# Softmax sums by three adding transfers a group in rotating buffers, with two small operations moved between engines

## The reference, cut to what matters

```python
q = (query @ Wq).reshape(b, sq, 32, 32).transpose(0, 2, 1, 3)
k = (key @ Wk).reshape(b, sk, 8, 32).transpose(0, 2, 1, 3)     # 8 heads, each serves 4 of q
v = (value @ Wv).reshape(b, sk, 8, 32).transpose(0, 2, 1, 3)
scores = jnp.einsum('bhqd,bhkd->bhqk', q, k) * scale            # 512 queries x 1024 keys a head
probs = jax.nn.softmax(scores, axis=-1)
out = jnp.einsum('bhqk,bhkd->bhqd', probs, v)
return out.transpose(0, 2, 1, 3).reshape(b, sq, 1024) @ Wo
```

## Time and profile before

| | us |
|---|---|
| median of 3 runs | 1242.94 (1241.52 to 1243.02) |
| the profiled execution | 1241.61 |
| its span, first to last instruction | 1239.8 |
| TensorE busy | 1208.2 (97%) |
| VectorE busy | 781.4 (63%) |
| GpSimd busy | 682.0 (55%) |
| ACT busy | 488.0 (39%) |
| mean granted clock of TensorE | 0.994 |

### The profile page before, as it was taken

The page is one execution under the profiler, slowest core; times in us unless marked ns, Lnnn a source line. Parts: engine busy times, 40 slices in busy tenths (PEclk is TensorE's granted clock), DMA queues, the critical chain, the costliest instruction groups (busy, mean ns, idle before and its releaser), DMA issues.

```text
span 1239.8 us, 16842 instructions
## 1 busy us (share of the span) xinstructions
PE 1208.2 (97%) x6358; PEld 511.8 (41%) x6440; DVE 781.4 (63%) x1303; ACT 488.0 (39%) x879; POOL 682.0 (55%) x300
## 2 busy tenths in 40 slices
PE   8999799999999999999999999999999999999998
PEld 6664344444444322222323233234444444444443
DVE  8898731433456788887878888145559846737622
ACT  4787421000110477776777777743252010010000
POOL 6006996500082188988999899860165543524500
PEclk9999899999999999999999999999999999999999
DMA  9577233311361145564656464533474343523301
GB/s 354 176 253 187 68 123 98 86 35 34 78 192 60 35 101 125 113 127 106 131 116 130 107 131 97 112 77 60 102 225 139 121 136 102 180 75 103 118 17 51
DMA packets 94302, 145.12 MB, mean 117 GB/s; under 512 B 54672, under 2 KB 64912, under 8 KB 90128
## 3 DMA queue, kind: packets, MB, share of 16 engines
q1 hardware_dynamic: 59712, 99.51, 25.8%
q0 software_dynamic: 4608, 33.56, 13.5%
q10 hardware_dynamic: 29904, 11.02, 4.0%
HBM read 89.16 MB, written 10.60 MB: 80 GB/s over the span
## 4 chain that ended last, share of the span: by engine, by line
PE 71%; POOL 11%; DMA 10%; DVE 5%; issue 2%; ACT 1%; SPq 0%; POOLq 0%; DVEq 0%; ACTq 0%
PE bank L706 48%; POOL R L672 7%; DMA stage_pair<-R 5%; PE bank L975 5%; PE bank L962 5%; PE bank L1007 4%; PE bank L1050 4%; DMA R<-R 3%; PE bank L755 3%; PE bank L724 2%; POOL stage_pair L672 2%; POOL xn L654 1%; DVE lnv L1548 1%; DMA XTl<-xn 1%; DMA stage_c<-ctx_t_in 0%
## 5 line engine op out<-in xcount | busy, mean ns | idle before, releaser
L1782 DVE TENSOR_REDUCE mxp<-bank 128x1 f32<-128x512 f32 x512 | 323.2, 683 | 86.1 <-PE bank L962 84.2
L1416 ACT ACTIVATE R<-bank 128x512 f32<-128x512 f32 x512 | 271.9, 602 | 107.9 <-PE bank L1050 103.2
L706 PE MATMUL bank<-XTh,R 128*128 128x512 bf16 x878 | 274.5, 380 | 3.2 <-DVE X L1830 2.3
L672 POOL TENSOR_TENSOR R<-R 128x2048 f32<-128x2048 f32 x48 | 222.3, 4631 | 79.1 <-ACT R L1416 51.1
L706 PE MATMUL bank<-R 128*128 128x512 bf16 x941 | 208.0, 379 | 1.1
L706 PE MATMUL bank<-XTl,R 128*128 128x512 bf16 x436 | 165.6, 380 | 0.8 <-issue 0.2
L694 POOL TENSOR_TENSOR R<-stage_pair,R 128x1024 bf16<-128x1024 f32 x32 | 75.7, 2382 | 130.0 <-DVE R L1940 69.4
L706 PEld LDWEIGHTS bank<-R 128*128 128x128 bf16 x960 | 93.9, 98 | 113.3
L975 PE MATMUL bank<-R,stage_c 128*32 128x512 f32 x1024 | 136.4, 604 | 0.7 <-ACT R L1416 0.7
L1050 PE MATMUL bank<-R 98*128 98x512 bf16 x352 | 133.9, 381 | 1.2 <-DVE R L1810 0.8
L962 PE MATMUL bank<-R 96*128 96x512 bf16 x352 | 134.4, 382 | 0.0
(11 more groups left out here) (202 smaller groups left out, 1428.3 us busy)
## 6 DMA issues: line engine op xcount, KB each, us to landing
stage_pair<-wts_in SPq DMA_DIRECT2D x35, 512.0 KB, 3.6
R<-R POOLq DMA_DIRECT2D x16, 1024.0 KB, 7.5
stage_pair<-R POOLq DMA_DIRECT2D x16, 1024.0 KB, 7.0
stage_pair<-w_in SPq DMA_DIRECT2D x32, 512.0 KB, 3.5
stage_c<-w_in SPq DMA_DIRECT2D x32, 512.0 KB, 3.6
R<-q_scr SPq DMA_DIRECT2D x48, 128.0 KB, 2.5
XTh<-ctx_t_in SPq DMA_DIRECT2D x11, 512.0 KB, 7.0
XTh<-ctx_nat_in SPq DMA_DIRECT2D x9, 512.0 KB, 4.2
```

Of the source, the lines that this page charges most:

```text
L672: pool.tensor_tensor(PS[(0, 1, 2, 1)[j]], PB[2 * j % 4], PB[2 * j % 4 + 1], ALU.add).then_inc(p_add, 1)
L706: mm = pe.matmul(o, a, m, start=first and a is ah and bs is bh, stop=last and a is al)
L1416: act.activation(PB[kt % 4][:, h * S:(h + 1) * S], bank[t_bank(g, t)][:, :], ACT.Exp, scale=float(HD) ** -0.5).then_inc(exp_done, 1)
L1782: dve.tensor_reduce(mxp[head // REP % 2][:, m, n // 2, n % 2:n % 2 + 1], bank[s_bank(u)][:, :], AX.X, ALU.max).then_inc(s_max, 1)
```

## The change: what it does

Sum buffers. The first buffer of a group, `total_in(g)`, is PS[0] for even groups; for odd groups it is a free stretch of another tensor (XTh's half of batch 1 for groups 1, 3, 5, 7, eight pieces of 1 KB a partition; half of `V` for 9 to 15). PS[1] and PS[2] take turns as `beside(g, 0)` and `beside(g, 1)`. Adds 0, 1, 2, 3 write total, beside 0, beside 1, beside 0. There are three adding transfers, all onto the total: the first after add 1, the second (of beside 1) just ahead of add 3, the third (of beside 0) after add 0 of the next group. So TensorE needs one product with ones a group, at step 30 of the next group; the last group still has two.

Moves. The copy of the values goes from GpSimd to ACT (step 12). The lower part goes from GpSimd to VectorE (step 10, for the group three before), the upper part from step 28 to step 4 of the next group. `divide` comes after add 2. `sums_in` is put behind the loads of the queries and keys in SP's queue, and `invert_few` goes from step 8 to 14. `junk`, a place for unused results, moves in `V`. The last three lower parts stay on GpSimd.

```diff
-TOTAL_AT = (2, 18)
-SUM_OUT_AT = 20
-FEW_AT = 8
-O_HI_AT = 28
+TOTAL_AT = 30
+SUM_OUT_AT = 31
+FEW_AT = 14
+O_HI_AT = 4
+VALUES_AT = 12
+O_LO_AT = 10
...
+        xth_1 = per_tile(XTh[:, :].bitcast(F32))[:, :, B * S // 4:B * S // 2]
...
+        def pieces(v):
+            return v.rearrange("p (k n) -> p k n", k=KT)
+        def total_in(g):
+            if g % 2 == 0:
+                return pieces(PS[0])
+            return xth_1 if g < KV_HEADS else pieces(V[:, 0:REP * S])
+        def beside(g, i):
+            return pieces(PS[1 + (g + i) % 2])
...
             for g in range(1, GROUPS):
                 rows_in(g)
-                if g >= 2:
-                    sums_in(g - 2)
                 if g + 2 < GROUPS:
                     sp.wait_ge(st_mm, STEPS * g)
                     queries_in(g + 2)
                     keys_in(g + 2)
+                if g >= 2:
+                    sums_in(g - 2)
...
+            def add_pair(g, j):
+                pool.wait_ge(exp_done, STEPS * g + 2 * REP * (j + 1))
+                if j == 0:
+                    if g >= 2:
+                        pool.wait_ge(one_mm, g - 1)
+                    dst = total_in(g)
+                elif j == 1:
+                    if g > 0:
+                        pool.wait_ge(ps_c, 16 * g)
+                    dst = beside(g, 0)
+                elif j == 2:
+                    if g > 0:
+                        pool.wait_ge(ps_d, 16 * g)
+                    dst = beside(g, 1)
+                else:
+                    pool.wait_ge(ps_b, 16 * (g + 1))
+                    dst = beside(g, 0)
+                pool.tensor_tensor(dst, pieces(PB[2 * j % 4]), pieces(PB[2 * j % 4 + 1]), ALU.add).then_inc(p_add, 1)
             for g in range(GROUPS):
                 for j in range(KT // 2):
-                    pool.wait_ge(exp_done, STEPS * g + 2 * REP * (j + 1))
                     if j == 3:
-                        pool.wait_ge(ps_sum[0], 16 * (g + 1))
-                    elif g > 0 and j == 1:
-                        pool.wait_ge(ps_sum[1], 16 * g)
-                    elif g > 0:
-                        pool.wait_ge(one_mm, 2 * (g - 1) + j // 2 + 1)
-                    pool.tensor_tensor(PS[(0, 1, 2, 1)[j]], PB[2 * j % 4], PB[2 * j % 4 + 1], ALU.add).then_inc(p_add, 1)
-                    if j % 2 == 1:
-                        pool.wait_ge(p_add, 4 * g + j + 1)
-                        pool.dma_start(PS[j - 1], PS[1], accum_op=ALU.add).then_inc(ps_sum[j // 2], 16)
-                    if j == 0 and 1 <= g < GROUPS - 1:
-                        stage_values(g + 1)
-                    if g >= 2 and j == 1:
+                        pool.wait_ge(p_add, 4 * g + 3)
+                        pool.wait_ge(ps_b, 16 * (g + 1))
+                        if g + 1 < GROUPS:
+                            pool.dma_start(total_in(g), beside(g, 1), accum_op=ALU.add).then_inc(ps_c, 16)
+                    add_pair(g, j)
+                    if j == 0 and g > 0:
+                        pool.wait_ge(p_add, 4 * g)
+                        pool.wait_ge(ps_c, 16 * g)
+                        pool.dma_start(total_in(g - 1), beside(g - 1, 0), accum_op=ALU.add).then_inc(ps_d, 16)
+                    if j == 1:
+                        pool.wait_ge(p_add, 4 * g + 2)
+                        pool.dma_start(total_in(g), beside(g, 0), accum_op=ALU.add).then_inc(ps_b, 16)
+                    if j == 3 and g + 1 == GROUPS:
+                        pool.wait_ge(p_add, 4 * GROUPS)
+                        pool.dma_start(beside(g, 1), beside(g, 0), accum_op=ALU.add).then_inc(ps_d, 16)
+                    if g >= 2 and j == 2:
                         divide(g - 2)
-                    if g >= 2 and j == 2:
-                        divided_lo(g - 2)
+            divided_lo(GROUPS - 3)
...
+            def over_pieces(weights, probs, first, last):
+                n = KT // REP
+                for h in range(REP):
+                    mm = pe.matmul(bank[6][h * HD:(h + 1) * HD, :].rearrange("p (k n) -> p k n", k=n), weights,
+                                   probs[:, h * n:(h + 1) * n, :], start=first, stop=last)
+                return mm
...
-            def total(g, j):
-                pe.wait_ge(ps_sum[j], 16 * (g + 1))
-                if j == 0 and g > 0:
+            def total(g):
+                if g > 0:
                     pe.wait_ge(sum_out, g)
-                over_keys(bank[6], onesf[:, 0:HD], PS[2 * j], j == 0, j == 1).then_inc(one_mm, 1)
+                if g + 1 < GROUPS:
+                    pe.wait_ge(ps_d, 16 * (g + 1))
+                    over_pieces(onesf[:, 0:HD], total_in(g), True, True).then_inc(one_mm, 1)
+                else:
+                    pe.wait_ge(ps_b, 16 * GROUPS)
+                    over_pieces(onesf[:, 0:HD], total_in(g), True, False)
+                    pe.wait_ge(ps_d, 16 * GROUPS)
+                    over_pieces(onesf[:, 0:HD], beside(g, 1), False, True).then_inc(one_mm, 1)
...
+            def values_staged(g):
+                act.wait_ge(pv_mm, KT * (g - 1))
+                b, kv = divmod(g, KV_HEADS)
+                src = V[:, b * KT * KVD:(b + 1) * KT * KVD].rearrange("p (t n) -> p t n", t=KT)
+                act.activation(VS[g % 2].rearrange("p (t n) -> p t n", t=KT), src[:, :, ds(kv, HD)], ACT.Copy).then_inc(vs_done, 1)
...
-                    if g > 1 and t == O_HI_AT:
-                        divided_hi(g - 2)
+                    if g > 2 and t == O_HI_AT:
+                        divided_hi(g - 3)
+                    if 1 <= g < GROUPS - 1 and t == VALUES_AT:
+                        values_staged(g + 1)
...
+            def divided_lo(g):
+                cols = o_cols(g)
+                dve.wait_ge(o_hi, g + 1)
+                dve.tensor_tensor(XTl[:, cols], onat, XTh[:, cols], ALU.subtract).then_inc(o_lo, 1)
...
+                    if g > 2 and t == O_LO_AT:
+                        divided_lo(g - 3)
```

More of the change, by code:

```diff
@@ L217, in build @@
         b2b = xn[0]
-        junk = V[:, 0:D // 2].bitcast(BF16)
+        junk = V[:, B * KT * KVD // 2:B * KT * KVD // 2 + D // 2].bitcast(BF16)
         stage_e = stage_w + stage_c
@@ L311, in build @@
         p_add = sem("p_add")
-        ps_sum = [sem(f"ps_sum{i}") for i in range(2)]
+        ps_b = sem("ps_b")
+        ps_c = sem("ps_c")
+        ps_d = sem("ps_d")
         one_mm = sem("one_mm")
@@ L634, in stage_values @@
             def stage_values(g):
-                if g >= 2:
-                    pool.wait_ge(pv_mm, KT * (g - 1))
                 b, kv = divmod(g, KV_HEADS)
@@ L1058, in group @@
                             weigh(g - 1, KT - 1)
-                    if g > 0 and t in TOTAL_AT:
-                        total(g - 1, TOTAL_AT.index(t))
+                    if g > 0 and t == TOTAL_AT:
+                        total(g - 1)
                     if STEPS * g + t >= STEPS * GROUPS - 6 * KT:
@@ L1096, in _ @@
             output_tile(1)
-            total(GROUPS - 1, 0)
-            total(GROUPS - 1, 1)
+            total(GROUPS - 1)
             pe.wait_ge(o_out, GROUPS)
@@ L1401, in sums_out @@
             def sums_out(g):
-                act.wait_ge(one_mm, 2 * (g + 1))
+                act.wait_ge(one_mm, g + 1)
                 if g > FEW_GROUPS:
@@ L1438, in _ @@
                 exp_group(g)
+            divided_hi(GROUPS - 3)
             outputs_out(GROUPS - 1)
```

## The result

The changed kernel takes 1296.9 us (median of 4 runs, 1291.7 to 1301.2) against 1243.0 (1241.5 to 1243.1) for the kernel before: ratio 1.0439, 95% interval 1.0411 to 1.0466. It is slower, as forecast and by the mechanism forecast, but by 54 us instead of 20: outside the range of 1234 to 1277. (Rival C of the prediction has numbers up to 1310, but from issues of 7 us and stalls of 4.6, and neither came; that the result lies there is chance.) The profiled execution took 1297.05 us, its span is 1295.2.

A forecast was written before the change was run, and what follows sets the result against it. TensorE, busy 97% of the span, was taken as the bound, GpSimd next. From 1241.6 us the terms -12.9 - 3 - 1 + 36.3 + 1 = +20.4 gave 1262.0; the 8-in-10 range was 1234 to 1277.

The forecast's parts named there:

- Rival C: GpSimd late but not enough, stalls of 4.6 us giving 1277; or issues in pieces dear, up to 1310; 7%.
- Rival A: VectorE's lower part at step 10 isn't held up and costs little: 1231 us; 10%.
- The clock behind the stalls: After step 13 of groups 3 to 13 TensorE idles some 3.3 us, its granted clock still full.
- The stall, 3.3 a group: TensorE stands 3.3 us while VectorE's lower part is held by addition 0, groups 3 to 13: +36.3 us.
- Rival B: GpSimd runs late, so VectorE's lower part falls between additions 3 and 0, unheld: 1235 us; 10%.
- Yes, on time, with 0.2 to spare: With the stall, GpSimd still finishes addition 3 just before the next group's addition 0 is due.
- Products with ones, -12.9: On TensorE in the attention loop, 15 products with ones saved at 0.86 us each: -12.9 us.
- Excess of the long windows, -3: Of 3.8 us by which four attention groups run long, rotating buffers remove 3 (between 0 and -3.8).
- "I take nothing" for the pieces: Adding transfers into 1 KB pieces, odd groups below 8, cost nothing extra to issue; high end 7 us.
- SyncE's order, 0: Moving `sums_in` behind the loads on SP's queue costs 0, the reciprocals landing with 1.3 us of cover.
- The two ends, -1 and +1: The last `total` no longer waits for a late transfer, -1 us; group 14's turn of maxima comes later, +1.
- Values on ACT, upper part: Copying values on ACT at step 12 costs 0; the upper part at step 4 makes exp(7) 0.2 us late.

The follow-up runs named there:

- e5: The kernel before with only the lower parts of groups 0 to 12 moved to VectorE at step 10, three groups later: 1287.6 us, ratio 1.0385.
- e14: The changed kernel with VectorE's lower part at step 22 instead of 10: 1250.0 us, ratio 1.0076.
- e3: The changed kernel with VectorE's lower part replaced by a maximum over one SBUF input, lower parts of groups 0 to 12 left out: 1254.6 us.
- e4: The changed kernel with twelve unread matmuls, 2.6 us, filling TensorE's stall behind step 13 in groups 3 to 13: 1286.8 us, ratio 1.0378.
- e6: e2 with the totals of groups 1, 3, 5 and 7 in 8 KB that lie together instead of pieces of 1 KB: 1246.9 us.
- e8: e6 with SyncE's loads of the next group's rows moved ahead of the wait for the reciprocals' landing: 1242.4 us, ratio 1.0013.
- e13: e8 with VectorE's lower part at step 22 instead of 14: 1241.2 us, ratio 1.0003.
- e7: e2 with the third adding transfer taken back for groups 0 to 14, and a second product with ones there instead: 1258.3 us, ratio 1.0127.
- e2: The changed kernel with VectorE's lower part at step 14 instead of 10: 1251.2 us, ratio 1.0087.
- e9: e8 with GpSimd's division moved behind addition 3, ACT's upper part to step 8 and VectorE's lower part to step 15: 1323.4 us.
- e11: e6 with single transfers for the few sums and for the reciprocals instead of four each, and `FEW_AT` 12: 1254.2 us, ratio 1.0103.

## Why the prediction was right or wrong

- **Direction and mechanism: right.** VectorE's lower part is held until GpSimd's addition 0 ends (3.64 us against 3.65); e5 and e14 show that it is this part and its step, and e3 with line 1656 that it is the second SBUF input. Rival A is refuted.
- **The clock behind the stalls: the step that failed.** It stood in the prediction as "TensorE idle some 3.3 us after step 13 of these groups and the granted clock still full". The term "11 x 3.3 = +36.3" was made of idle time alone. Measured: 29.3 us more from matmuls at 1.2 GHz, in 13 stretches. e4 gives groups of 27.0 at full clock, where the change has 28.4 to 29.6. 21.4 us were forecast for the loop, 57.9 came; the difference is 31.6 of longer busy time (29.3 of it the clock) and 4.9 of idle time. The Trainium skill, "TensorE: Matmul & The Clock Gate", section "HAM oscillation — how this bites in real kernels", says that a TensorE which idles between bursts comes back at the half rate and pays anew each time. The trace agrees (0.54 in the window behind the stall), and I had not weighed that page against an idle gap that repeats in every group.
- **The stall, 3.3 a group: near.** TensorE's gaps at the holds are 1.7 to 3.5 us, 31 in all for the 36.3 forecast; e5 has 2.73 in ten groups and 3.07 in one.
- **The hold's length: too short in some groups.** Where GpSimd was late, VectorE's instruction came at the very end of one addition and was held through the whole of the next, as here:

```profile
499.98 4.82 POOL L698 TENSOR_TENSOR R<-R 128x2048 f32<-128x2048 f32 x1
504.48 4.77 POOL L698 TENSOR_TENSOR XTh<-R 128x2048 f32<-128x2048 f32 x1
...
504.18 5.63 DVE L1833 TENSOR_TENSOR XTl<-xn,XTh 128x512 bf16<-128x512 f32 x1
```

  Rival B had VectorE slip in between additions 3 and 0. The second addition was queued right behind the first, and VectorE got no turn between them; its row ends 0.56 us after the second (509.25). Four of the 13 rows are such, of 5.6 to 6.4 us. Where the next addition came later, VectorE got its turn (the last row, 2.0 us). "Yes, on time, with 0.2 to spare" did not hold in groups 3, 4, 6 and 14. Groups 4 and 6 come behind groups whose totals stand in pieces; what made GpSimd late for 3 and 14 was not looked into.
- **Products with ones, -12.9: right.** e14 has windows of 23.92 us with TensorE busy throughout, where the earlier trace rows has 24.77; the 0.86 of the earlier trace rows is there.
- **Excess of the long windows, -3: wrong.** The cause named, a landing in 9.2 us, did not go: with a third transfer the DMA engines are busy for 0.59 to 0.83 of the groups after the first instead of 0.56, and in e6, e8 and e13, without pieces and nearly without holds, 15 to 16 us of idle time are left against 5.1.
- **"I take nothing" for the pieces: mis-sized.** 0.7 to 1.0 us an issue and 1.7 us a landing; about 4 us of the kernel (e6). "If the adding transfers of odd groups take longer to issue" was one of its own signs of being wrong, and they do.
- **SyncE's order, 0: mis-sized.** The rows, issued last, were waited for (5.5 us in e6), and with them first the kernel took 4.5 us less (e8). The keys, issued beside the second transfer, were waited for too: 7.7 us in the change, nothing before. The cover of 1.3 us for the reciprocals was gone at times: GpSimd waited 2.2 us for them in the change (446 to 810) and 7.2 in e6.
- **The two ends, -1 and +1: near.** The last product with ones no longer waits for a transfer (0.96 us before), and TensorE waits 0.8 us for the turn of the maxima in group 14.
- **Values on ACT, upper part: right,** as far as seen: no wait in the rows for them. They were not run alone.

What stays open: why 13 stretches are of 3.4 us in some groups and of 6.8 in others, and how much of the 15 us of idle time in e6, e8 and e13 is the third transfer's (e7 against e2 says 6 to 8 us of its gain are lost).

## What to carry to other kernels

An idle gap of the bounding TensorE is to be priced twice: the gap, and the slower matmuls behind it. Here 2.7 us of gap cost 1.6 to 3.0 more, in ten groups of 11 (e5). Before an elementwise operation with both inputs in SBUF goes to VectorE beside long GpSimd work, find a step at which GpSimd stands (step 22 instead of 10: 47 us). A subtraction with one input in PSUM and a maximum over one input in SBUF were not held; a cast of one input in SBUF was. And when a step is moved later, ask who waits for its buffer (e9), and which traffic its old place may have kept apart (e11).

## Not expected of the hardware

- VectorE is passed over when a second GpSimd instruction is queued behind the first: 5.63 us for 0.65 of work, in four rows of 13.
- The clock fell after gaps as short as 0.96 and 1.67 us with 1.04 us of matmuls between them (688.72 to 691.43), but stayed full behind one gap of 2.73 us in e5. With matmuls in the gap it stays full in eight of the 11 groups (e4).
- The same 1 MB added from SBUF to SBUF in pieces of 1 KB takes 9.5 us to land and 1.58 of that to issue, in whole 8 KB 7.8 and 0.87, with the same loads beside it: 0.8 us (medians) more behind the issue. The Trainium skill, "DMA: Bandwidth & Descriptors", section "Why small descriptors are slow (HBM only)", says that transfers between SBUF places have no such penalty. For these adding ones the measurement decides.
- With one spread of 256 KB behind it an adding transfer took 10.7 us to land, with four of 64 KB 7.9 (e11 against e6; two other edits went with it).
